# Layer-norm statistics of the w_d stage, issued two output chunks later than their own

## The reference, cut to what matters

```python
_layernorm(x) = (x - mean(x)) / sqrt(var(x) + 1e-5)       # over the last axis, D = 1024

# attention block, x is [4, 4096, 1024]
h = layer_norm(x, ln1_g, ln1_b)
q, k, v = h @ wq, h @ wk, h @ wv                          # 4 heads of 256
x1 = x + linear_attn(q, k, v) @ wo + bo
h = layer_norm(x1, ln2_g, ln2_b)
x2 = x1 + gelu(h @ w_ff1 + b_ff1) @ w_ff2 + b_ff2
a  = x2 @ w_d + b_d

x = _layernorm(x + a)                                     # "LN3" below
gate, up = x @ (w_gate/127).T, x @ (w_up/127).T           # 3072 wide
x = _layernorm(x + (silu(gate) * up) @ (w_down/127).T)    # "LN4" below
```

## Time and profile before

| | before |
|---|---|
| median of 3 runs (lowest, highest) | 2018.06 us (2015.64, 2021.14) |
| profiled execution, device time | 2019.74 us |
| its span, slowest core (core 5) | 2018.1 us |
| spans of the 8 cores | 2012.4 to 2018.1 us |
| PE busy | 1648.0 us, 82% |
| DVE, ACT, POOL busy | 28%, 24%, 6% |
| mean granted TensorE clock, core 5 | 0.890 |

### The profile page before, as it was taken

How to read it: one execution, slowest core, us unless ns; L and a number is a source line. 1 busy time by engine, 2 the same in 40 slices (tenths; PEclk the granted TensorE clock), 3 DMA queues, 4 the chain that set the end, 5 groups by cost and what they waited for, 6 DMA issues and landing times.

```text
span 2018.1 us, 20608 instructions; the slowest of 8 cores (2012.4 to 2018.1 us)
## 1 busy us (share of the span) xinstructions
PE 1648.0 (82%) x7096; PEld 679.3 (34%) x7096; DVE 566.3 (28%) x880; ACT 481.5 (24%) x750; POOL 130.7 (6%) x140
## 2 busy tenths in 40 slices
PE   1488888996748768999999966557999999999674
PEld 0133333442212223444444421112344444444121
DVE  1643333302113522403021122324213213322223
ACT  1233333322324324030312300222210110011422
POOL 0000000000000230000000000222100000000113
PEclk9998888998887769999999986668899999999766
DMA  9221110020074320222211061001004004000112
GB/s 187 68 55 54 57 42 1 1 42 0 1 130 121 51 34 7 36 42 42 42 42 42 1 124 43 27 15 42 1 0 126 1 1 125 1 0 1 42 42 83
DMA packets 47636, 89.58 MB, mean 44 GB/s; under 512 B 1328, under 2 KB 5552, under 8 KB 47536
## 3 DMA queue, kind: packets, MB, share of 16 engines
q1 hardware_dynamic: 30896, 61.01, 10.1%
q0 software_dynamic: 16640, 27.26, 9.4%
HBM read 107.14 MB, written 8.39 MB: 57 GB/s over the span
## 4 chain that ended last, share of the span: by engine, by line
PE 53%; DVE 5%; ACT 4%; POOL 4%; DMA 3%; issue 2%; DVEq 0%; POOLq 0%; ACTq 0%; SPq 0%
PE pb L888 11%; PE pb L862 10%; PE pb L1092 8%; PE pb L1102 8%; PE pb L1145 8%; PE pb L1002 4%; DMA estR<-xkv 3%; PE pb L788 2%; POOL R L960 2%; ACT sbb L640 2%; ACT sbb L649 1%; PE pb L655 1%; POOL sbb L634 1%; DVE R L1012 1%; DVE R L1054 1%
## 5 line engine op out<-in xcount | busy, mean ns | idle before, releaser
L1092 PE MATMUL pb<-h2x,W 128*128 128x512 bf16 x768 | 184.8, 384 | 3.4 <-ACT slbt L1111 3.4
L1145 PE MATMUL pb<-Dr,wslotE 128*128 128x512 bf16 x768 | 176.6, 394 | 8.9 <-DVE R L1152 8.9
L1102 PE MATMUL pb<-h2x,W 128*128 128x512 bf16 x768 | 183.3, 382 | 0.0
L869 ACT ACTIVATE Gq<-pb,pv 128x512 bf16<-128x512 f32 x128 | 88.0, 687 | 312.1 <-PE pb L862 311.4
L651 PE MATMUL pb<-sbb,cb 128*1 128x512 bf16 x96 | 51.4, 537 | 123.2 <-ACT sbb L640 51.4
L1111 ACT ACTIVATE slbt<-pb 128x512 bf16<-128x512 f32 x96 | 57.3, 597 | 369.8 <-PE pb L1092 366.1
L1116 DVE SCALAR_TENSOR_TENSOR Dr<-slbt,pb 128x512 bf16<-128x512 bf16 x96 | 66.0, 688 | 273.9 <-PE pb L1102 260.3
L903 DVE TENSOR_TENSOR R<-R,pb 128x512 f32<-128x512 f32 x96 | 66.0, 687 | 265.5 <-PE pb L888 265.5
L418 PE MATMUL pb<-W,h 128*128 128x512 bf16 x512 | 127.2, 393 | 0.4 <-ACT ebf L426 0.4
L862 PE MATMUL pb<-h2x,W 128*128 128x512 bf16 x512 | 120.9, 401 | 7.3 <-ACT Gq L869 6.0
L434 PE MATMUL pb<-slotD,h 128*128 128x512 bf16 x512 | 121.6, 380 | 0.0
(11 more groups left out here) (98 smaller groups left out, 1474.5 us busy)
## 6 DMA issues: line engine op xcount, KB each, us to landing
xq<-xkv SPq DMA_DIRECT2D x8, 2048.0 KB, 10.9
estR<-xkv SPq DMA_DIRECT2D x32, 256.0 KB, 3.4
W<-wff POOLq DMA_DIRECT2D x4, 2048.0 KB, 20.9
slotD<-wff POOLq DMA_DIRECT2D x4, 2048.0 KB, 18.2
estR<-xkv SPq DMA_DIRECT2D x4, 2048.0 KB, 12.5
y<-xq SPq DMA_DIRECT2D x4, 2048.0 KB, 7.3
W<-wgT SPq DMA_DIRECT2D x3, 2048.0 KB, 9.6
W<-wuT SPq DMA_DIRECT2D x3, 2048.0 KB, 15.6
```

Of the source, the lines that this page charges most:

```text
L869: se = b.op("scalar", lambda e, jj=jj, t=t, qq=qq, bk=bk: e.activation(Gq[:, jj * NOWN + t * NT: jj * NOWN + (t + 1) * NT], bk["ap"][:, :] ...
L1092: b.op("tensor", lambda e, hc=hc, kc=kc, t=t, bA=bA: e.matmul(bA["ap"][:, :], W0[:, kc * 1024 + hc * 128: kc * 1024 + (hc + 1) * 128], h2x ...
L1102: b.op("tensor", lambda e, hc=hc, kc=kc, t=t, bB=bB: e.matmul(bB["ap"][:, :], W1[:, kc * 1024 + hc * 128: kc * 1024 + (hc + 1) * 128], h2x ...
L1145: b.op("tensor", lambda e, m=m, hc=hc, t=t, wds=wds, bk=bk: e.matmul(bk["ap"][:, :], wds[:, hc * 1024 + m * 128: hc * 1024 + (m + 1) * 128 ...
```

## The change

In tiles 0 to 2, `stats_c(m - 2)` is issued at step `m` in place of `stats_c(m)`, with a wait for the evacuation of its own chunk, whose count is kept in `ve_hist`. `stats_c(6)` and `stats_c(7)` follow the loop. Tile 3 keeps its order. No instruction is added or dropped, and no engine of an operation changes.

```diff
@@ -992,6 +992,7 @@
+        ve_hist = [0] * CH
         for m in range(CH):
@@ -1015,13 +1016,17 @@
             Pool.rel(bk, "ve", ve)
-            if t < 3:
-                L3[t]["stats_c"](m, xw=[("ve", ve)])
+            ve_hist[m] = ve
+            if t < 3 and m >= 2:
+                L3[t]["stats_c"](m - 2, xw=[("ve", ve_hist[m - 2])])
             if m == 4 and t >= 1:
                 l3_apply(t - 1)
         u_evac[t] = b.cnt["ve"]
         Pool.rel(slot, "ve", u_evac[t])
-        if t == 3:
+        if t < 3:
+            L3[t]["stats_c"](6, xw=[("ve", ve_hist[6])])
+            L3[t]["stats_c"](7, xw=[("ve", ve_hist[7])])
+        else:
             for c in range(CH):
                 L3[3]["stats_c"](c, xw=[("ve", u_evac[3])])
```

## The result

The changed kernel takes 1968.5 us (median of 10 runs), the kernel before 2019.8 us (10 runs), ratio 0.974, 95% interval 0.971 to 0.977. Forecast: 1964, range 1954 to 1986.

The account below looks back on a forecast made before the run. Tiles 0 to 2 of the w_d stage were taken as bound by a chain through the engines, with PE waiting for casts. Gains 18.4 + 18.2 + 19.2 = 55.8 us from 2019.7 gave 1963.9, forecast 1964, range 1954 to 1986.

Parts of the forecast that it names:

- The step: Tiles 0 to 2: cast and one hand-over leave the chain; a plain step takes 3.81 us full clock, 5.72 half.
- second rival: Tiles 0 to 2: the whole wait goes, a step about 2.2 us at the full clock, time 1942; chance 0.04.
- The end of a tile: Step 7, with the last squares and cast queued on DVE: 5.5 us at the full clock, 7.6 at the half.
- Tile 0: First tile of the w_d stage: three groups done before x lands, end at 1232.0, gain 18.4 us.
- Tiles 1 and 2: w_d stage: a broadcast wait and a hole behind l3_apply remain; 38.0 and 37.0 us, gains 18.2 and 19.2.
- The clock: PE in tiles 0 to 2: leans to the full level after the change, from means of 0.63 to 0.68.
- first rival: Tiles 0 to 2: clock stays mostly at the half level, gain 30 to 43 us, time 1975 to 1988; chance 0.26.
- The row the forecast leaned on: Pairs of matmuls at 560 us: PE busy 3.81 of 5 us, clock 1.00 throughout, gaps shorter than 1.3.
- the prediction's signs: Trace marks of right or wrong: among them tile 0's mean clock over 0.8 if right, tile 3 over 32 us if wrong.
- The slower rival: Holes behind l3_apply: DVE and POOL blocks and copies don't overlap, 13.3 us more each, time 2028; chance 0.03.
- half-clock gain: Whole kernel, with PE all at the half clock: gain 30.4 us, time 1988.
- The sum: Gains of tiles 0, 1 and 2: 18.4 + 18.2 + 19.2 = 55.8 us off the profiled 2019.7.

Follow-up runs that it names:

- sq_first: The changed kernel with the deferred statistics issued ahead of the newest evacuation, so DVE's square stands before it: 1944.6 us.
- split_apply: The changed kernel with l3_apply issued two chunks at a time at steps 4 to 7, not in one block: tiles 1 and 2 take 41.9 and 41.6 us.

## Why the prediction was right

- **The bound** was a chain through the engines in tiles 0 to 2: all of the gain is there, and less than 1 us of it came back, in tile 3 (the clock, below).
- **The step.** 3.81 and 5.72 us were forecast from rows of other steps, 3.81 and 5.71 were measured; the square starts 0.10 behind the evacuation (1228.75 to 1228.85). sq_first shows by its 2.14 that nothing else held L655, and is by itself the second rival (about 2.2 a step), which for the changed kernel failed for the reason given.
- **The end of a tile.** Forecast 5.5 at the full clock; 1229.73 to 1235.20 is 5.47.
- **Tile 0.** Group 3 was to start 3.67 behind the first evacuation; 1207.19 to 1210.84 is 3.65. x landed later on this core (17.4 us after the first group, not 15.7), and nearly two steps ran at the half clock, not one: 45.4 us on this core and 43.9 as a median, where 42.8 (1189.2 to 1232.0) was forecast. Here the forecast was 1.1 us short.
- **Tiles 1 and 2.** Forecast 38.0 and 37.0, measured 38.3 and 37.2. The broadcast L698 starts 5.46 into tile 1 (forecast 5.6), and the wait at chunk 3 is 5.72 ("nearly 6"). L655 of chunk 3 is 26.1 into the tile where 25.5 was forecast: group 2 started 0.3 earlier than forecast, and the cast and square behind `l3_apply` took 1.0 longer (last section). In tile 2 the forecast's wait of 0.8 for the broadcast didn't come; the two groups ahead of it took 4.9 us and not 3.5, because they ran in part at the half clock.
- **The clock**, the largest unknown, went mostly as forecast: 0.77 to 0.87 against 0.63 to 0.68, at the half level behind the two long waits and at the full one in the steps between. The first rival would have kept the steps at 5.7; the trace shows the full clock held over gaps of 1.30, as in tile 1 from 1240.97 to 1254. The row the forecast leaned on, with shorter gaps, did not prove this; the run does, so that the choice of the full level was in part luck. By the rule that the prediction takes from the Trainium skill's page "TensorE: Matmul & The Clock Gate", section "A second HAM failure mode: psum-queue depth-cycling", the short gaps alone would have gone on moving the clock; in the steps with one gap of 1.30 the trace does not agree. Two of the prediction's signs were missed by a little: in tile 0 the mean clock is 0.77 on this core (0.74 to 0.84 among the cores), not over 0.8, and tile 3 takes 32.3. The forecast had overlooked a third place at the half level, the end of a tile with its short waits. The first 16 matmuls of tiles 2 and 3 took 4.86 and 5.05 us, where those of tile 1 took 3.63.
- **The slower rival** asked for 10 us more per hole in which both blocks add up. They run side by side, 0.9 us apart. split_apply is what comes nearest to it: there the same blocks are entered four times, and cost 4 us a tile. The rival's price was worked out wrongly: it counted the hole of tile 3, whose order does not change. With two holes it is 26.6 us more and not 40, and 15 us per hole, not 10, would have been needed to undo the half-clock gain.
- **The sum.** 55.8 us forecast, 54.8 in the tiles, 51 in the median of the runs. Of the 4.5 between forecast and result (1964 and 1968.5), 1 us is in the tiles' medians, and 0.7 went back in tile 3. The rest lies in which core ends last. The mean of the eight spans fell by 54.9 us (2016.3 to 1961.5), that of the slowest core by 51.5 (2018.1 to 1966.6): before, tiles 0 to 2 took 173.5 to 174.4 us on the cores with complete records, now they take 115.6 to 122.2, and the three cores that end last (3, 7 and 4) are the three with the longest, 121.7 to 122.2. The forecast had every core gain what one core gains.

## What to carry to other kernels

Software pipelining across in-order engines moves a wait only as far as each queue allows: after delaying a consumer by two steps, read every engine's order for what now stands ahead of the delayed work. Here one of three instructions stayed behind the newest evacuation, and moving two lines gave another 21 us in the tiles. Count the clock in as well, at both of its levels: at least about 30% of this gain (16 of 54.8 us) was matmuls that ran at the full clock because PE idled less. And a block of side work that runs once beside two groups can be cheaper than the same work spread evenly, if the spread puts a hand-over between engines into every step.

## What the runs showed of the hardware

A bf16 square on DVE takes 0.42 us. Behind `l3_apply`, while POOL multiplies, the same square took 1.19 (1259.98 to 1261.17, above), and the cast ahead of it took 0.64 instead of 0.43 (1259.24 to 1259.88). POOL's multiplications take 1.15 each, and ACT's L964 starts 0.15 behind each of them, which tells where they ended (1259.6 and 1260.9):

```profile
1259.74 0.63 ACT L964 ACTIVATE h2x<-R 128x512 bf16<-128x512 f32 x1 [0.67 <-POOL R L960]
1261.04 0.63 ACT L964 ACTIVATE h2x<-R 128x512 bf16<-128x512 f32 x1 [0.67 <-POOL R L960]
```

Both DVE instructions started while a multiplication ran, and both ended 0.28 us after it, whatever was left of it. The other way round, POOL's cast takes 0.61, and 0.75 where it starts while DVE's square runs, in sq_first, core 3:

```profile
1208.97 0.42 DVE L643 TENSOR_TENSOR sbb<-sbb 128x512 bf16<-128x512 bf16 x1
1209.12 0.75 POOL L634 CAST sbb<-R 128x512 bf16<-128x512 f32 x1 [1.75 <-DVE R L1015]
```

The fp32 subtractions, with one operand in PSUM, took 0.69 beside the same multiplications, as all 32 of the kernel do, and showed none of it. The Trainium skill's page "SBUF — State Buffer", in the section "SBUF: two separate sides", says that DVE and GpSimd share one pair of ports that works as an exclusive lock, and that a DVE instruction with two SBUF inputs or in a 2-port mode is blocked for the whole of a GpSimd instruction that holds it. The trace agrees, though it doesn't show whether the cast ran in such a mode: the instruction that started second was the longer one, and the end of its wait goes by the end of the other's instruction. It cost 1.0 us at the hole of tile 1 (0.21 in the cast, 0.77 in the square) and 0.8 at that of tile 2, where the square alone was lengthened.
